# Cross-attention kernel: byte-wide even heads, unread transposes, 128-row keys, and finishing tiles inside the loop

## The reference

```python
q = (x @ Wq + bq).reshape(1, B * N, H, hd)            # H = 16 heads of hd = 16
kv = (cond @ Wkv + bkv).reshape(1, -1, 2, H, hd)      # 1024 keys
q = _fq_sym(q * scale, axis=-1); k = _fq_sym(k, axis=-1); v = _fq_sym(v, axis=2)
attn = softmax(einsum('bhqd,bhkd->bhqk', q, k))
attn = _fq_unsigned(attn, axis=-1)     # round(attn / (max / 255)): integers 0..255
out = einsum('bhqk,bhkd->bhqd', attn, v)
x = x + (out @ Wp + bp)
x = x + (einsum('bsi,oi->bso', layernorm(x), ternary_quantize(weight)) + bias)
```

## Time and profile before

| | us |
|---|---|
| median of 3 runs | 338.5 (337.76 to 339.55) |
| the profiled execution | 337.5 |
| its span, first to last instruction | 335.7 |
| PE busy | 268.7 (80%) |
| DVE busy | 265.7 (79%) |
| ACT busy | 210.0 (63%) |
| POOL busy | 98.3 (29%) |
| mean granted TensorE clock | 0.65 of full speed |

### The profile page before, as it was taken

One profiled execution on the slowest core, in us unless ns is written; L12 is line 12 of the kernel. 1 busy time (PEld: TensorE's weight loads), 2 busy tenths in 40 slices (PEclk: granted clock), 3 DMA queues, 4 the chain that ended last, 5 costly groups with the idle time before them and its releaser, 6 DMA issues.

```text
span 335.7 us, 5142 instructions
## 1 busy us (share of the span) xinstructions
PE 268.7 (80%) x1728; PEld 127.3 (38%) x1728; DVE 265.7 (79%) x401; ACT 210.0 (63%) x340; POOL 98.3 (29%) x225
## 2 busy tenths in 40 slices
PE   4993597595156947899999999999999999979670
PEld 4441365473034733233333332333333333338560
DVE  3363799968697878999999899899999999973850
ACT  1100125435533178999999999999999999992210
POOL 2350424476603011221222212222222122211634
PEclk9999559987555977555555555555555555558998
DMA  7824000039100001999999999999999999995011
GB/s 255 276 94 126 0 3 0 0 59 161 34 0 0 0 2 37 196 182 206 185 200 178 215 172 212 184 212 164 227 167 219 197 188 190 199 184 109 16 49 63
DMA packets 148618, 43.34 MB, mean 129 GB/s; under 512 B 143216, under 2 KB 147696, under 8 KB 148592
## 3 DMA queue, kind: packets, MB, share of 16 engines
q1 hardware_dynamic: 146496, 39.60, 65.4%
q0 software_dynamic: 768, 2.10, 1.8%
q10 hardware_dynamic: 1328, 1.32, 1.2%
HBM read 5.25 MB, written 2.10 MB: 22 GB/s over the span
## 4 chain that ended last, share of the span: by engine, by line
issue 36%; DVE 18%; PE 17%; POOL 16%; ACT 6%; DMA 6%; POOLq 1%; ACTq 0%; DVEq 0%
POOL ebias L421 8%; PE ps L1175 5%; PE ps L1158 4%; PE ps L1047 3%; DMA ksplit<-in_x 3%; DVE nmax L878 2%; ACT ctxT L566 2%; POOL scratch L369 2%; PE ps L1150 2%; POOL rstd L375 2%; POOL xs L432 2%; DMA xs<-scratch 2%; POOL out L446 1%; DVE stats L850 1%; ACT kv L557 1%
## 5 line engine op out<-in xcount | busy, mean ns | idle before, releaser
L878 DVE TENSOR_REDUCE nmax<-ps 128x1 f32<-128x1024 f32 x128 | 156.3, 1224 | 16.5 <-PE ps L1175 11.6
L1175 PE MATMUL ps<-keysT,kv 64*128 64x512 bf16 x256 | 130.1, 614 | 9.2 <-ACT ctx L566 1.9
L566 ACT ACTIVATE ctx<-ps,ebias,qscale 128x1024 int16<-128x1024 f32 x64 | 76.9, 1203 | 5.4 <-POOL ebias L421 3.5
L566 ACT ACTIVATE ctxT<-ps,ebias,qscale 128x1024 int16<-128x1024 f32 x64 | 77.0, 1203 | 4.0 <-POOL ebias L421 2.5
L1204 PEld LDWEIGHTS ps<-vals,ksplit 128*128 128x128 f16 x1024 | 36.9, 105 | 100.6 <-issue 100.3
L421 POOL TENSOR_SCALAR ebias<-nmax,qcur 128x1 f32<-128x1 f32 x128 | 33.8, 264 | 136.2 <-DVE nmax L878 127.2
L1204 PE MATMUL ps<-vals,ksplit 128*128 128x16 f16 x1024 | 47.7, 176 | 0.8 <-DVE krest L923 0.8
L475 ACT COPY hT<-ps 128x256 f32<-128x256 f32 x11 | 4.1, 372 | 46.5 <-PE ps L1039 46.5
L1175 PEld LDWEIGHTS ps<-keysT,kv 64*128 64x128 bf16 x256 | 16.3, 107 | 21.8 <-ACT ctx L566 8.1
L543 ACT COPY hT<-ps 128x512 f32<-128x512 f32 x8 | 4.7, 586 | 22.5 <-PE ps L1150 22.5
L1022 PE MATMUL ps<-wkv_s,ctxT 128*128 128x512 f32 x32 | 16.4, 668 | 0.7 <-ACT ctxT L469 0.7
(11 more groups left out here) (176 smaller groups left out, 316.1 us busy)
## 6 DMA issues: line engine op xcount, KB each, us to landing
ctx<-in_ctx SPq DMA_DIRECT2D x2, 512.0 KB, 4.9
ksplit<-in_x ACTq DMA_DIRECT2D x1, 1024.0 KB, 10.9
xs<-scratch SPq DMA_DIRECT2D x1, 1024.0 KB, 5.6
wkv_s<-in_L_xattn_Wkv SPq DMA_DIRECT2D x1, 512.0 KB, 8.1
ksplit<-ctx SPq DMA_TRANSPOSE x32, 4.7
ksplit<-ctxT SPq DMA_TRANSPOSE x32, 4.9
bkv_b<-in_L_xattn_bkv ACTq DMA_DIRECT2D x1, 256.0 KB, 11.4
wt_s<-in_L_ffn_weight SPq DMA_DIRECT2D x1, 256.0 KB, 9.4
```

The lines of the kernel that those rows point to most:

```text
L566: a.activation(prob_of(w)[:, (u % 2) * NK:(u % 2 + 1) * NK], score_banks(k, u), ACT.Exp, bias=ebias[:, u % 4:u % 4 + 1], scale=qscale[:, t ...
L878: v.tensor_reduce(nmax[:, u % 4:u % 4 + 1], score_banks(k, u), AX.X, ALU.max, negate=True).then_inc(max_ready, 1)
L1175: last = m.matmul(ps[:, bank + b, :], qT[rows, t, u // 2, :], keysT[rows, u // 2, 512 * b:512 * b + 512], start=True, stop=True)
```

## The change

1. `keysT` gets two copies of the keys, each with 128 partitions. In copy 0 the odd heads' half is zero, in copy 1 the even heads' half. SP issues 16 DMA transposes for 8, and POOL zeroes the unused halves with 16 memsets, before the roots for the third norm. The score matmuls now contract over 128 rows.
2. Even heads' exp writes bytes, odd heads' still int16; a pair has 1536 16-bit columns for 2048. ACT reads the even head's scores so that keys 128 apart lie side by side in the bytes. After the transpose the bytes of two keys, 128 apart, share one 16-bit word, and POOL unpacks them with one copy a pair (1024 elements, `unpack`, six heads behind) into `byteT`.
3. `weigh` is seven heads behind, and ahead of each stand four bf16 transposes of the identity (FILLERS = 4) into half of a bank that nobody reads. There is one output bank (`PV_BANK`) for all tiles.
4. The tile's finishing goes into the loop, one tile at a time. For tile t - 1: PE turns its output at u = 9, ACT copies at u = 10, PE projects at u = 11 (the bias is now a matmul of one row), DVE adds at u = 14 and takes the sums at u = 15, POOL takes the root at u = 15. For tile t - 2: POOL normalizes at u = 1 and 3, PE turns at u = 4, ACT copies at u = 5, PE multiplies at u = 6, DVE adds at u = 9, POOL scatters at u = 13. Behind the loop remain tile 6's second half and tile 7.
5. `qcur` and POOL's addition to `xs` go. Some temporaries share memory (`wtemps`, `gates`).

The core of the diff:

```diff
+WEIGH_LAG = 7
+FILLERS = 4
...
             for r in range(KT):
-                sp.dma_start_transpose(keysT[:, :, r * P:(r + 1) * P],
+                for a in range(2):
+                    sp.dma_start_transpose(keysT[:, a, :, r * P:(r + 1) * P],
...
+            pool.wait_ge(vn_ready, 1)
+            for r in range(KT):
+                pool.wait_ge(keys_turned[r], 32)
+                for a in range(2):
+                    if r + a:
+                        pool.wait_ge(keys_zeroed, 2 * r + a)
+                    other = slice(P // 2, P) if a == 0 else slice(0, P // 2)
+                    g.memset(keysT[other, a, :, r * P:(r + 1) * P].bitcast(F32), 0.0).then_inc(keys_zeroed, 1)
...
+            def unpack(t, u):
+
+                pair_turned(pool, t, u // 2)
+                if not (first_tile(t) and u < 2 * PT):
+                    pool.wait_ge(pv_done, count(*before(t, u, 2 * PT)))
+                g.tensor_copy(byteT[:, (u // 2) % PT, :, :, :],
+                              rawT[:, (u // 2) % PAIRS, 0:KT // 2, :].bitcast(U8).rearrange(
+                                  "p b (q j) -> p b j q", j=2)).then_inc(unpacked, 1)
...
-                a.activation(prob_of(w)[:, (u % 2) * NK:(u % 2 + 1) * NK], score_banks(k, u), ACT.Exp,
+                if u % 2 == 0:
+                    probs = prob_of(w)[:, 0:NK // 2].bitcast(U8).rearrange("p (b q j) -> p b q j", q=P, j=2)
+                    s_in = score_banks(k, u).rearrange("p (b j q) -> p b q j", j=2, q=P)
+                else:
+                    probs, s_in = prob_of(w)[:, NK // 2:PW], score_banks(k, u)
+                a.activation(probs, s_in, ACT.Exp,
...
             def attention(t, k):
                 for u in range(H):
                     head_exp(t, k, u)
+                    if u == 5 and t >= 2:
+                        copy_h4(t - 2)
+                    if u == 10 and t >= 1:
+                        copy_att(t - 1)
...
+                    if u == DIVIDE_AT + 1 and t >= 2:
+                        add_ternary(t - 2)
+                    if u == H - 2 and not first_tile(t):
+                        add_projection(t - 1)
+                    if u == H - 1 and not first_tile(t):
+                        fourth_sums(t - 1)
...
-                rows = slice(u % 2 * P // 2, (u % 2 + 1) * P // 2)
                 for b in range(2):
-                    last = m.matmul(ps[:, bank + b, :], qT[rows, t, u // 2, :], keysT[rows, u // 2, 512 * b:512 * b + 512],
+                    last = m.matmul(ps[:, bank + b, :], qT[:, t, u // 2, :], keysT[:, u % 2, u // 2, 512 * b:512 * b + 512],
                                     start=True, stop=True)
...
+                if fillers:
+                    idle = ps[:, PV_BANK, D:2 * D].bitcast(BF16)
+                    for i in range(FILLERS):
+                        m.transpose(idle[:, i * P:(i + 1) * P], identb[:, :], identb[:, :])
...
+                m.matmul(out, onesf[0:1, :], bias[0:1, :], start=True, stop=False)
+                for c in range(C):
+                    last = m.matmul(out, lhs[:, t % 2, c, :], w[:, c, :], start=False, stop=(c == C - 1))
...
-                    if u >= WEIGH_LAG:
+                    if u == WEIGH_LAG + 1:
+                        weigh(t, k, 0)
+                    if u > WEIGH_LAG:
                         weigh(t, k, u - WEIGH_LAG)
-                    elif not first_tile(t):
+                    elif u < WEIGH_LAG and not first_tile(t):
                         weigh(t - 1, k - 1, u - WEIGH_LAG + H)
+                    if t >= 2:
+                        if u == 4:
+                            h4_turn(t - 2)
+                        if u == 6:
+                            ternary(t - 2)
+                    if t >= 1:
+                        if u == 9:
+                            att_turn(t - 1)
+                        if u == 11:
+                            project(t - 1)
```

More of the change, by code:

```diff
@@ L424, in attention @@
             def attention(t, k):
[L425 to L428 removed]
                 for u in range(H):
                     exp_bias(t, u)
[L431 to L434 removed]
+                    if u % 2 == 0 and not (first_tile(t) and u < UNPACK_LAG):
+                        unpack(*before(t, u, UNPACK_LAG))
@@ L455, in _ @@
-            for g2 in range(1, NG):
-                scatter_output(g2)
+            for c in range(C):
+                fourth_norm(NT - 2, c)
+            for u in range(H - UNPACK_LAG, H, 2):
+                unpack(NT - 1, u)
+            scatter_output(NT - 2)
+            fourth_root(NT - 1)
+            for c in range(C):
+                fourth_norm(NT - 1, c)
+            scatter_output(NT - 1)
             pool.wait_ge(stored, 16 * NT)
@@ L1205, in weigh, with turn_tile, product_tile @@
                                     start=(r == 0), stop=(r == KT - 1))
                 last.then_inc(pv_done, 1)
+            def turn_tile(src, t, out, full):
+                for c in range(C):
+                    last = m.transpose(out[:, c * P:(c + 1) * P], src[:, t, c * P:(c + 1) * P], identf[:, :])
+                last.then_inc(full, 1)
+            def product_tile(lhs, w, bias, t, out, full):
+                m.matmul(out, onesf[0:1, :], bias[0:1, :], start=True, stop=False)
+                for c in range(C):
+                    last = m.matmul(out, lhs[:, t % 2, c, :], w[:, c, :], start=False, stop=(c == C - 1))
+                last.then_inc(full, 1)
```

253 lines of the change are left out of this document (126 added, 127 removed).

## The result

| | before | after |
|---|---|---|
| median (lowest to highest) | 338.9 us (337.8 to 339.6, 4 runs) | 348.8 us (346.8 to 349.5, 4 runs) |
| ratio after / before | | 1.029, 95% interval 1.023 to 1.034 |
| profiled execution, its span | 337.5, 335.7 us | 349.5, 347.7 us |
| mean granted clock | 0.65 | 0.845 |

The account below looks back on a forecast made before the run. The prediction took a ring of TensorE, ScalarE and VectorE, none at 100%, to bound the kernel. Attention +12.2 and tail -9.5 gave +2.7 on 337.5, so 340.2 profiled and a median of 341; range 326 to 354 us.

Parts of the forecast that it names:

- a ring at 1.20 us a head: Attention loop: scores, maximum, bias and exp wait on each other in turn; 1.20 us a head at 2.4 GHz, now 1.347.
- +12.2: Attention loop, first exp to end of last: 185.4 us after the change for 173.2 before, so 12.2 us longer.
- -9.5: Tail behind the last exp: 23.9 us for 33.4, so 9.5 us shorter.
- The clock rises with the transposes: Attention loop: 128-row keys and fillers raise TensorE to 2.4 GHz from head 8 of tile 0, with odd dips.
- the low clock: Rival for the attention loop: clock stays at 1.2 GHz, 1.7 us a head, +75 us, 413 us in all; 7%.
- Unpacking 1.1 us, bytes at no cost on ScalarE, clearing .6, 16 key transposes landed by 96: Loop: POOL copy 1.1 us a pair, byte exps 0 extra; ahead of it: memsets about 0.6 each, transposes landed by 96.
- A tile of 23.3: Middle tile of the attention loop: 19.2 + 1.0 + 1.2 + 1.7 + 0.2 = 23.3 us against 21.7 before.
- Copies 1.0 and unpacking .2 a tile: Per loop tile: two ACT copies hold exps up 1.0 us; unpacking makes biases late, about 0.2 us.
- The other tiles: Attention loop: tile 0 22.6 us, tile 1 22.5, the last 22.8, where five take 23.3.
- Ahead of the loop nothing, at worst +2: Before the first exp: 16 key transposes and 16 memsets stay hidden with 2 to 3 us to spare; 0, at worst +2.
- Tail 23.9: From the end of the last exp to the kernel's end: 23.9 us, at the low clock; near 20 with it up.
- The rival that bursts fit in: Rival for the loop: products and additions fall into waiting time, tiles 21.0 to 21.4 us, 327 us in all; 30%.

Follow-up runs that it names:

- the best version: Changed kernel with finishing work behind the loop, clearing on ScalarE, unpacking in halves, unread transposes from the first head, last tile's chain moved ahead: 326.0 us, ratio 0.966.
- the version with halves: Changed kernel with finishing work behind the loop, clearing on ScalarE, early unread transposes, and unpacking in two halves, one behind each bias: 329.5 us, ratio 0.976.

## Why the prediction was near, and where it was off

**The sign** was right, and the mechanism of the loop in its main lines too: a ring at 1.20 us a head in undisturbed heads, and a product that holds up a score pair. But the forecast sign came of a small difference between +12.2 and -9.5. The three stretches were each forecast too low, by 3.3, 2.5 and 3.5 us on the profiled execution, and none made up for another; that the time is still in the range is owed to the range's width of 28 us. Step by step:

- *The clock rises with the transposes.* Right for this kernel, for a reason that was half of it. I named both the keys and the transposes, but argued the rise from a burst of transposes at 126 us alone, and used the half-array scores only to set the low clock aside. The kernel before with the transposes alone stayed at .50. Of what was run, only transposes and whole-array scores together kept it up. The Trainium skill, "TensorE: Matmul & The Clock Gate", Part 4 (PE-mode transpose), says that the full clock doesn't engage for transposes, which are not counted as busy in the same way. The run with transposes and half-array scores agrees with it; the changed kernel against its version without them does not (.91 against .73 in 200 to 260 us). I gave the low clock 7%; what saved the step was the other half of the change.
- *Unpacking 1.1 us, bytes at no cost on ScalarE, clearing .6, 16 key transposes landed by 96.* Measured 1.036, 1.204, .587 and 94.6.
- *A tile of 23.3.* It was 23.97. The product was under-priced: six instructions at .215 from the earlier trace rows gave 1.3 us, and they take 1.59 (211.57 to 213.16). The two of line 1275, with a contraction over one row, take .31 each and not less than the others; the four of 1277 .24. In the gaps of tile 3 above 1.20 us, exps 9 and 10 are late by 1.4 (forecast 1.2), and exps 14 and 15 and the next tile's first by 2.0 (1.7).
- *Copies 1.0 and unpacking .2 a tile.* Their sum, 1.2, came out nearly right, by luck: what is left of the tile's lateness is 1.4, and 1.0 of that is the unpacking, since four exps a tile wait for it by .26 each. The .2 does not even follow from my own words: eight biases a tile, each .2 late, and that halved, are .8. The copies were over-priced instead: the first holds exp 6 up by .28, the second stands ahead of an exp that waits for its bias anyway. The norm on GpSimd was longer than seen ahead (.80 for each half), but costs nothing in the loop (the kernel without it: 23.96 to 24.00).
- *The other tiles.* Tile 0 21.5 for 22.6 (the clock came up earlier, .84 over the tile; the heads that I listed add up to 22.9, not 22.6), tile 1 23.0 for 22.5. The sum was 2.5 us too low.
- *Ahead of the loop nothing, at worst +2.* Wrong, and the largest miss for its size. I asked only whether GpSimd would be done in time; it was (100.3). The step that failed is "hidden": I priced the clearings on their own queue and not by what they do to VectorE. Eight rounding instructions took 5.8 us (3.1 + 2.7) instead of 3.0: 2.8 of the 3.3 us. (Three versions with the same clearings had their first exp at 128.9 to 129.1 all the same, since they came to the rounding 1.4 to 1.6 us earlier and lost less behind it. The 3 us are clear only from the rounding on, over all traces.)
- *Tail 23.9.* It was 27.4. From the end of the last exp (320.24), in the changed kernel:

```profile
320.28 1.58 POOL L486 TENSOR_SCALAR hs<-xs,mv,rstd 128x128 f32<-128x128 f32 x2
321.83 2.01 POOL L462 CAST gates<-ksplit 128x1024 int16<-128x1024 uint8 x2
...
324.05 1.04 POOL L462 CAST gates<-ksplit 128x1024 int16<-128x1024 uint8 x1 [0.21 <-DMA ksplit<-ctxT]
324.35 0.67 PE L1270 MATMUL ps<-identf,hs 128*128 128x128 f32 x2
...
325.47 1.22 PE L1275 MATMUL ps<-bt_b,onesf 1*128 1x256 f32 x2 [0.46 <-ACT hT L637]
326.62 2.07 PE L1277 MATMUL ps<-wtT,hT 128*128 128x256 f32 x4
328.49 0.41 PE L1263 MATMUL ps<-vals,gates 128*128 128x16 f16 x8
```

  The last pair is unpacked at 325.1 and weighed at 328.5, behind the ternary product of the tile before, as foreseen, but the divide ends .9 later than forecast. The last tile's two products take 3.2 us each at the lower clock, not 2.8 (together .8), its norm 1.6, not .9 (.7), and the .5 that I took off for overlaps was not there; .2 more lies behind the last scatter. That is 3.1 of the 3.5; the rest are gaps between the steps.
- *The rival that bursts fit in* gave 327, at a TensorE step under 1.2 us with a product in it. The step with the product in it is 2.5 us (from scores at 210.63 to the next at 213.16). The rival's time, 327, is nearly that of the best version, but that one gets there by other means: it has no products in the loop.

## What to carry to other kernels

In a ring of engines, work that "fits into idle time" by the busy shares fits only if each piece is shorter than the slack at its place in the queue. Here a tile fell from 21.65 to 20.83 us with the faster clock and the bytes, and 3.1 us went back to the finishing work, most of it around products that stand in one piece ahead of scores. An unpacking of 1.04 us between two biases was too long in the same way, and halving it gained nothing on average, since another bias was then held up. Price an instruction that moves to GpSimd also by what VectorE does at that moment, not only by its own queue. And an experiment that takes an engine's work out (here 1.7 us a tile of GpSimd's, for nothing) tells a hidden cost from a paid one, where the list of busy times can't.

## What the runs showed of the hardware

- **Clock.** Half-array scores (64 rows) with transposes and TensorE busy 59.97 of 60 us: granted clock .50 throughout 200 to 260 us. Whole-array scores without the transposes: .73 in the same window, going up and down. Both: .91 to 1.00. TensorE was busy for 50.60 of the 60 us at .91, less than at .50.
- **VectorE beside GpSimd.** VectorE's instructions with one input from SBUF took .82 us for .42 (f32), .72 for .42 (int32), .69 for .41 and 1.65 for 1.22 beside GpSimd's clearings; those with two f32 inputs stayed at .68, and clearings on ScalarE disturbed nothing. The Trainium skill, "SBUF — State Buffer", section "Who interferes with whom", has VectorE's two-port instructions and GpSimd share one pair of ports as an exclusive lock. The longer times agree with it if these instructions run in such a mode, which no trace shows; I had not looked it up for this step.
- **Unpacking bytes** on GpSimd costs 1.04 us for 1024 elements, and .61 for 512 in the version with halves.
